# A decoder in two interleaved lanes: the order of the lanes' steps made anew, with one lane held back from its first feed-forward stage

## What is computed

```python
x = _layernorm(x + _L0_attn_ref(x, ...))               # attention over groups of 4 tokens
x = _layernorm(x + _L0_xattn_ref(x, ctx, ctx, mask0))  # cross-attention, 77 context tokens, 16 heads
x = _layernorm(x + _L0_ffn_ref(x, ...))                # one adapter of 8, picked for a sequence
x = _layernorm(x + _L1_attn_ref(x, ...))               # "bump" attention, 16 heads
x = _layernorm(x + _L1_xattn_ref(x, ctx, ctx, mask1))  # cross-attention, other mask
x = _layernorm(x + _L1_ffn_ref(x, ...))                # 2 x (causal self-attention + mixture of experts)
```

## Time and profile before

| | |
|---|---|
| time, median of 3 runs | 1280.47 us |
| the 3 runs | 1280.47, 1270.23, 1284.65 us |
| the profiled execution, its own time | 1281.58 us |
| its span from the first to the last instruction | 1279.8 us |
| PE busy | 1035.3 us (81%) |
| DVE busy | 758.0 us (59%) |
| ACT busy | 643.5 us (50%) |
| PE weight loads busy | 603.7 us (47%) |
| POOL busy | 390.9 us (31%) |
| granted TensorE clock, mean | 0.870 |

### The profile page before, as it was taken

How to read it: one execution, slowest core, us unless ns; L and a number is a source line. 1 busy time by engine, 2 the same in 40 slices (tenths; PEclk the granted TensorE clock), 3 DMA queues, 4 the chain that set the end, 5 groups by cost and what they waited for, 6 DMA issues and landing times.

```text
span 1279.8 us, 20162 instructions
## 1 busy us (share of the span) xinstructions
PE 1035.3 (81%) x7286; PEld 603.7 (47%) x7286; DVE 758.0 (59%) x1949; ACT 643.5 (50%) x1254; POOL 390.9 (31%) x773
## 2 busy tenths in 40 slices
PE   7858786888889689589897777797779869859986
PEld 6754431234444389344464431243334459824454
DVE  2754566677695531596455557777597641388353
ACT  2114369854237456137643368863326636415751
POOL 4032130243124522424312122323224431523520
PEclk8878868788789989789998788888789989978999
DMA  8023000210430056530112200102340026470011
GB/s 292 18 58 67 20 4 1 59 48 20 110 98 2 22 165 197 142 100 3 35 58 70 56 11 4 51 10 60 101 105 3 4 97 200 117 194 15 3 51 33
DMA packets 71147, 86.54 MB, mean 68 GB/s; under 512 B 18720, under 2 KB 59472, under 8 KB 70544
## 3 DMA queue, kind: packets, MB, share of 16 engines
q1 hardware_dynamic: 68136, 80.57, 22.1%
q0 software_dynamic: 2048, 4.20, 1.2%
q10 hardware_dynamic: 864, 0.48, 0.1%
...
## 4 chain that ended last, share of the span: by engine, by line
PE 31%; DVE 14%; ACT 5%; POOL 5%; issue 5%; DMA 4%; SPq 1%; POOLq 0%; DVEq 0%; ACTq 0%
PE banks L1433 4%; PE banks L1421 3%; ACT sb_arena L1311 3%; PE banks L1408 3%; DVE sb_rmax L1562 2%; PE banks L1886 2%; POOL sb_region L1745 2%; PE banks L1659 2%; PE banks L1876 2%; PE banks L1673 2%; PE banks L977 1%; PE banks L624 1%; DMA sb_region<-done,sb_region 1%; PE banks L489 1%; PE banks L1261 1%
## 5 line engine op out<-in xcount | busy, mean ns | idle before, releaser
L1562 DVE TENSOR_REDUCE sb_rmax<-banks 128x1 f32<-128x512 f32 (+3 forms) x352 | 207.1, 634 | 72.3 <-PE banks L1410 71.3
L1491 ACT ACTIVATE sb_arena<-banks 128x512 f32<-128x512 f32 x320 | 176.4, 597 | 110.0 <-PE banks L1421 108.5
L1408 PE MATMUL banks<-sb_arena,sb_qs 128*128 128x384 bf16 (+3 forms) x512 | 133.9, 334 | 39.7 <-DMA sb_arena<-k_scratch 20.5
L1311 ACT ACTIVATE sb_arena<-banks,sb_zk 128x512 f32<-128x512 f32 x256 | 151.9, 732 | 11.9 <-PE banks L1261 8.9
L1517 POOL TENSOR_SCALAR_AFFINE_SELECT sb_arena<-sb_arena 128x256 f32<-128x256 f32 x256 | 99.3, 410 | 186.4 <-ACT sb_arena L1491 185.9
L1421 PE MATMUL banks<-sb_qs,sb_arena 128*128 128x512 bf16 (+3 forms) x512 | 109.5, 306 | 11.9 <-DVE sb_rmax L1562 3.9
L479 POOL TENSOR_SCALAR sb_var<-sb_mv 128x4 f32<-128x4 f32 x40 | 14.2, 354 | 342.2 <-DVE sb_mv L464 342.2
L1053 ACT ACTIVATE sb_arena<-banks 77x512 f32<-77x512 f32 x128 | 73.2, 590 | 73.6 <-PE banks L966 56.2
L1357 DVE TENSOR_SCALAR sb_arena<-sb_arena,sb_bw 128x2048 f32<-128x2048 f32 x64 | 89.4, 1408 | 29.8 <-ACT sb_arena L1311 29.5
L1408 PEld LDWEIGHTS banks<-sb_arena,sb_qs 128*128 128x128 bf16 x512 | 49.3, 106 | 105.7 <-DVE sb_rmax L1562 41.4
L1410 PE MATMUL banks<-sb_trib,sb_identb 128*128 128x128 bf16 (+2 forms) x352 | 93.6, 266 | 0.0
...
## 6 DMA issues: line engine op xcount, KB each, us to landing
...
```

Source lines behind the costliest of these rows:

```text
L1311: i = nc.scalar.activation(L.dist[h % 3][:, kb, :], (b2_, b3)[h % 2], ACT.Abs, bias=L.zk[:, kb, h:h + 1])
L1408: nc.tensor.matmul(o[:, i * kl:(i + 1) * kl], L.qs[:, h // 2, t * 128:kl], L.ks[:, key_of(h), 0:kl], start=(i == 0), stop=False)
L1491: nc.scalar.activation(L.probs[:, u % SLOTS, :], bank_of(SELF_ORDER, ring, ("key", u)), ACT.Exp)\
L1562: nc.vector.tensor_reduce(L.rmax[:, t, g * GROUP + h0:g * GROUP + h0 + nh], bank_of(SELF_ORDER, ring, ("max", step))[:, 0:nh * kl] .rearra ...
```

## The change

Only the table `ORDER` is changed, in all five numbers. No instruction is added or taken away, no wait and no buffer changes: the same steps are mixed in another order. Lane 1 is held back before its F0 of the first round. The numbers are equal up to shortly before that stage, and their last part, from about the first steps of S0 of the second round on, is nearly equal again. Two lines of the diff:

```diff
     "SP":
-    "2855d94e600ff901fd5606c2bf80fd5660063bdcf801ff8077cb81a8afe03f95998",
+    "2855d94e600ff8037f2e03527f80fea66006f74f3801ff8077cb81a8afe03f95998",
...
```

More of the change, by code:

```diff
@@ L184 @@
-    "fdfecffffffffffff90012a00005ca1524944894aa22413d2384a4a4929231e02aadfffefeffdfffeff7fffa88c0001eaaaa"
-    "fffffc00854001ffaaa22515492583370555a9292694c9e0124ca488fc05ecbefffff7fbfffa0480a7fffc",
+    "803783cf2700004cc33de3f187803800600f00031bbfffffffffbb00000421104abeeff8cc00c35b08d60180000000003f80"
+    "001fb7bb7fff79fefffffffffffe744004540002aaa925224a15511109a5386094925244780aabbfff7dfeffffbfdfffffe2"
+    "44280007d55ffffff0022a0007ff5544b5428cc555438aaaac4a49d2984a4a4929318f80cb5efffffefdfff1201aabf95e00"
@@ L186 @@
+    "00902000007000f007e00078dfbfffff7ff7fffffdd1442040012227ef7f830030dcc237005000000ffffe438010000399df"
+    "ffff77f9fffffffffc0025400015710a925421455491049d2384a4a4929231e02aadfffefeffdfffeff7fffa88c0001eaaaa"
+    "fffffc008a8001ffaaa22515492583370555a9292694c9e0124ca488fc05ecbefffff7fbfffa0902a9fffc",
     "ACT":
-    "c03cd9001ffe01f082020706fffffd2a081086f3003fe286ffc0038080effdd80003fffffffe000007f024a52a548a020eff"
-    "7f7fffff2000f6affe00003ffff800003f80a529529450083bff7f7ffe7c87f200304420ffc00007eefbfffdf404440df500"
@@ L189 @@
-    "3fe3446ffc0001c05fed80003fffffffff8000001fc09515494a0305ff7f7fffffa2003dabff80000ffffe0007f029555549"
-    "454a2a0307bffdfffa047fe",
+    "c03cd9001ffe01f082040706fffffc8001122fc801ff8d11ffe000000efec0000ffffff80ffffc00003f80a92948a0306ff7"
+    "effffffe42003dbffe00003ffff8007f02aa9955291525480707dffdffe889fe000c1ffc0000000fbffdfdffd248004afa80"
+    "1fe3446ffc01c0203bfeb80003ffffffff8000003f811515494a0305ff7f7fffffa2003dabff80000ffffe0007f029555549"
+    "454a2a0307bffdfffa093fe",
     "POOL":
-    "81e38d8e600fce60003fffe000000ffe01c1998670c003f7ffdbdffe0ff8008001fffffe000007ff001cc199870c003f7fff"
@@ L193 @@
[L193 removed]
+    "81e38d8e600cfd0000f800fffc0003ff8003e06618007f7ffcf66fffcff8008001fffffe0007ff00e30ccce30c330c003ffb"
+    "ffff81ce725e00cfe60003fffe0000003ff8009e19867000fdfff6defff0ff8008001fffffe0007ff001c333319c30c3000f"
     "fefffff98",
     "DVE":
[L196 to L197 removed]
@@ L198 @@
-    "0844425109902078001ff6eb97dfe36dbfffd46880d55006b55555b557fffea5d83ff868407900d4a803fed56b55556955ff"
-    "f803fc81fe",
+    "003f00fe1f8b800aa5be000001fffffff802be4000c9aeae8ba091108a42640800007f7bd73b7ede3cffffd851a1035540ba"
+    "aaab5aabfffeb2ee0ffd18901e406a9400ffdb5b56aaa9555ffe01bf80e1e0020a8000007fd7d73fffff83378c9500765b16"
+    "844442510990207ff8001fae73bf7e6dfff8f1a101aaa00d5aaaaadaabfffea5d83ff868407901aa5003fed56b55556955ff"
+    "f805fd01fe",
 }
```

7 lines of the change are left out of this document (removed).

## The result

| | before | changed |
|---|---|---|
| time, median of 4 runs each | 1276.13 us | 1295.93 us |
| range of the runs | 1270.23 to 1284.65 | 1295.71 to 1301.23 |
| the profiled execution, its own time | 1281.58 | 1295.72 |
| its span | 1279.8 | 1293.9 |
| granted TensorE clock, mean | 0.870 | 0.869 |

The ratio is 1.0144 with a 95% interval of 1.0098 to 1.019: the changed kernel is 1.4% slower, some 18 us. A second measurement on another chip gave 1.0151 (1.0113 to 1.0189). The forecast was 1287.5 us, with "within 1%" as the likeliest outcome. The measured time lies inside the whole range of 1265 to 1306, but that range spanned three rivals. It is 2 us above the forecast's own range (1281 to 1294, chance 0.40) and inside rival B's (1293 to 1310), and it is slower by over 1%, to which 0.29 was given.

A forecast was written before the change was run, and what follows sets the result against it. ACT was taken to bound the bump stages, chains through engines and DMAs X0 and M1. Terms 3 to 6 gave +7 on 1281.6, so 1288.6, against the median 1287.5; own range 1281 to 1294, whole range 1265 to 1306.

The forecast's parts named there:

- rival B: Clearly slower: a low PE clock makes single-lane heads, and scores behind a PE hole, slower; 1300 us, chance 0.20.
- Term 1: First round, start of lane 0's heads: they start earlier, 0 to -1.2 us, taken as -1.
- Term 2: First-round hand-over between lanes' heads: ACT holes grow, +4.2 us; lane 1's X1 about 3 us later, lane 0's 1 earlier.
- The +1 carried to S1: First round, S0 to S1: the lanes' mean shift of +1 us carried on as 0 to +1.
- Terms 3 to 5: First round's end to second round's heads: lane 0's X0 +10 us, PE idle some 7, heads +12 to +13.
- Term 4: X0 of the second round: lane 1 starts 2.5 us later, but its last matmul comes 2 us earlier.
- Term 6: Second-round hand-over: ACT holes fall from 7.7 to some 2.5 us, -5.2.
- A: Faster: lane 1's expert matmuls fill the PE hole where lane 0 opens S1; about 1272 us, chance 0.18.
- Rival C: No effect: the two rounds only swap roles, hand-over holes moving from second to first; 1282 us, chance 0.22.

The follow-up runs named there:

- f0_back: The changed kernel with only lane 1's F0 of the first round back at its old place, ahead of lane 0's heads; 1.0107 of the kernel before.
- r1_bump: The kernel before with the changed order only from the start to lane 1's entry into X1 of the first round; 1290.73 us against 1280.44, ratio 1.0106.
- to_s1: The kernel before with the changed order only from the start to the opening of S1 of the first round; ratio 1.0176.
- after_again: The changed kernel measured once more, nothing altered; 1.0151 of the kernel before.
- from_s1: The kernel before with the changed order from the opening of S1 of the first round to the start of X1 of the second; ratio 1.0103.
- old_bump: The changed kernel with the start up to lane 1's entry into X1 of the first round put back as before; 1.0153 of the kernel before.
- r2_tail: The kernel before with the changed order only from X1 of the second round to the end; ratio 0.9967, and 0.9979 when repeated.

## Why the prediction was right or wrong, step by step

**The reading of what bounds the kernel** held. ACT's work in the bump stages is the same, and the stretch grows by its holes alone.

**Term 1** (first heads 1 us earlier) didn't show: 174.95 against 173.92. Lane 0's X0 and F0 ended 2.2 us later already, and L1244 came 1.8 us behind L484, not 2.9; the gain that I saw is there and is eaten before. Over all profiles the first head comes at 173.1 to 177.0 us with the old order and 174.2 to 176.4 with the new, so this term is within the scatter.

**Term 2, the hand-over, is the step that failed.** It put +4.2 on lane 1, -1 on lane 0's X1, and the mean of +1 on the kernel. Measured: +13 and +8 at X1 in the one pair, +10 and +5.5 over all profiles. Its price for the chain itself was right, since f0_back has 7.9 us of holes. Its baseline was not: the holes before were 2.34 + 3.26 = 5.6 us, and 3.26, not 2.34, was the largest. Two more sentences of it were wrong:

- "Holding lane 1's F0 back costs nothing in itself: its steps have 16 heads to hide behind." They were placed behind the tenth, with six heads left, and their end is awaited by L484: 2.7 to 3.0 us of hole at L1295 in the changed kernel, r1_bump, to_s1 and after_again, and 0.24 in f0_back. How much of this reaches the end isn't shown.
- "Lane 0's X1 starts 59.8 us after the first head, whatever stands at the hand-over." That it was 59.8 twice was chance: with the same order it is 56.3 to 61.3, by the clock. It is 67.0 in the changed kernel, 62.7 in r1_bump (237.69 less 175.00) and 58.5 in f0_back. That is some 6 us at a like clock (62.7 against 56.4, 66.5 against 60.9), of which f0_back gives back about 4 by moving F0 alone.

The low clock (0.50 from 218 to 233) makes 3.2 of the 13.9 us of holes, and it is low there in most profiles of the old order too, so it explains little of the difference. I had considered the clock only for the single lane's heads, where it was indeed 1.00 again (190 to 204), and had not put it on the hand-over. The page of the Trainium skill that the prediction names ("TensorE: Matmul & The Clock Gate", section "A second HAM failure mode: psum-queue depth-cycling") says that small idle times between groups can make the clock swing; the changed kernel's trace has such a swing over 204 to 235, where the mean is 0.61. In f0_back it falls among the single lane's heads too, and PE then needs 1.94 + 0.61 = 2.55 us for a head where ACT needs 2.37, just as rival B had it:

```profile
193.84 1.94 PE L1261 MATMUL banks<-sb_arena 128*32 128x512 f32 x8 [1.47 <-ACT sb_arena L1311]
196.19 0.61 PE L1252 MATMUL banks<-sb_k,sb_selb 128*128 128x512 bf16 x1 [0.41 <-ACT sb_arena L1311]
```

It lasts from 193.2 to 200.0 (0.50) and costs ACT one hole of 0.34 us. Whether short idle times are the cause, no run here separates. Rival B named the range in which the time fell, but its mechanism is worth at most some 4 us, not 18.

**The +1 carried to S1** was the second error: I let S0, M0 and S1 average the lanes, and gave X1 no price at all, though its order is new as well. The shift arrived whole and grew, +11 and +16 at S0, +14 and +14 at S1. Over all profiles lane 0 enters S0 at 312.0 us and lane 1 at 340.1 with everything old, and at 321.4 and 355.9 in the three with F0, BU and X1 new (+9 and +16).

**Terms 3 to 5** were right in mechanism. The hole on PE that ends just ahead of lane 0's first L941 is 5.95 us (forecast some 7), this L941 comes 16.2 us after its L484 (forecast 15), and the heads start 16.6 us after lane 1's L489 (forecast 15). Lane 0 entered X0 at 685.12, that is 6.5 us more than the shift at S1, where +10 was forecast. Term 4 was too small: lane 1's X0, from its L484 to its L489, takes 56.2 us (forecast 62.7).

**Term 6** was right: one hole of 2.28 us is left at the second hand-over (2.5 us were forecast in all), and the stretch is shorter by about 4 us. Summed, I gave this half +7; the profile of the changed kernel shows about 0 for it, from_s1, which has it without the last part, +13 (7 to 20). Which of the two it "costs" depends on what stands before it.

**The rivals.** A: no. Where lane 0 opens S1, PE is busy for 9.3 of 21.3 us, as before. C: half; the rounds did swap their hand-overs as forecast, but the new one costs more than twice what the old one gives back (+12 against -4 us on the two stretches, in the one pair). Rival C's range and mine both rested on adding terms, which such an order doesn't allow.

**What stays open.** That the order up to the opening of S1 makes the loss is shown by to_s1. How it shares out between F0 and BU on one side and X1 to M0 on the other isn't: with F0 and BU alone new the time is 1.1% longer (r1_bump), with all but them new 1.5% (old_bump), and X1 to M0 was not run alone. Nor is it shown why X1 takes longer in its new order, beyond the wait in old_bump. Why the middle part costs 1% behind the old first half and nothing behind the new one was not followed row by row. No version beat the kernel before by more than its measurement is uncertain; r2_tail came nearest, 0.9967 and 0.9979.
